# Half of the turned probabilities made by a transposing DMA, exponentials in place over the scores, and weights stored by panel

## The reference

```python
q = (x @ Wq + bq).reshape(1, B * N, H, hd)             # 512 queries, 16 heads of 64
kv = (cond @ Wkv + bkv).reshape(1, -1, 2, H, hd)       # 8192 keys and values
k, v = (kv[:, :, 0], kv[:, :, 1])
q = _fq_sym(q * scale, axis=-1)                        # round to 127 levels per row
k = _fq_sym(k, axis=-1)
v = _fq_sym(v, axis=2)
attn = softmax(einsum('bhqd,bhkd->bhqk', q, k))
attn = _fq_unsigned(attn, axis=-1)                     # round to 255 levels of the row's largest
out = einsum('bhqk,bhkd->bhqd', attn, v)
x1 = out @ Wp + bp
```

## Time and profile before

| What | us |
|---|---|
| Median of three runs | 3053.57 |
| The profiled execution | 3055.36 |
| Its span | 3053.5 |
| Busy: PE, DVE, ACT, POOL | 2747.3, 1967.6, 1139.9, 552.6 |
| Attention, first copy of scores to last output | 1457.32 to 2280.03 |

### The profile page before, as it was taken

How to read it: one execution, slowest core, us unless ns; L and a number is a source line. 1 busy time by engine, 2 the same in 40 slices (tenths; PEclk the granted TensorE clock), 3 DMA queues, 4 the chain that set the end, 5 groups by cost and what they waited for, 6 DMA issues and landing times. The chain is left out here.

```text
span 3053.5 us, 47748 instructions
## 1 busy us (share of the span) xinstructions
PE 2747.3 (90%) x18856; PEld 1408.6 (46%) x18856; DVE 1967.6 (64%) x3074; ACT 1139.9 (37%) x1240; POOL 552.6 (18%) x208
## 2 busy tenths in 40 slices
PE   6999999999999999995788888888867999499998
PEld 3444444444444444443455555555544457244443
DVE  5855555555555555553899999999976344366663
ACT  3111111111111111110699999999983134111100
POOL 0400000000000000000663635353601551001100
PEclk9999999999999999998899999999998986799999
DMA  6122122222122222214323242424213300300000
GB/s 228 62 76 82 57 73 82 82 79 79 65 72 76 82 82 76 73 64 118 104 57 112 57 112 57 112 56 112 57 40 136 111 28 1 59 14 14 8 1 28
DMA packets 241147, 220.14 MB, mean 72 GB/s; under 512 B 137457, under 2 KB 203249, under 8 KB 238193
## 3 DMA queue, kind: packets, MB, share of 16 engines
q1 hardware_dynamic: 241008, 218.06, 22.9%
HBM read 115.28 MB, written 69.21 MB: 60 GB/s over the span
## 5 line engine op out<-in xcount | busy, mean ns | idle before, releaser
L455 PE MATMUL kv_acc<-kv_whi,kv_xthi 128*128 128x512 f16 x2048 | 777.2, 379 | 6.1 <-DVE kv_xtlo L499 6.1
L455 PE MATMUL kv_acc<-kv_wlo,kv_xthi 128*128 128x512 f16 x2048 | 777.2, 379 | 0.0
L455 PE MATMUL kv_acc<-kv_whi,kv_xtlo 128*128 128x512 f16 x2048 | 777.1, 379 | 0.0
L851 DVE TENSOR_SCALAR_CACHE_REDUCE at_sc<-at_score 128x1024 f32<-128x1024 f32 x512 | 608.1, 1217 | 57.7 <-PE at_score L778 57.7
L934 ACT ACTIVATE at_prob<-at_sc,at_bias,at_qs 128x2048 uint16<-128x2048 f32 x256 | 535.2, 2090 | 28.0 <-DVE at_bias L863 26.3
L778 PE MATMUL at_score<-at_kt,at_q 128*128 128x512 f16 x1024 | 317.5, 396 | 141.3 <-DVE at_sc L851 92.2
L486 ACT ACTIVATE kv_parts<-kv_key 128x1024 f16<-128x1024 f32 x64 | 67.7, 1058 | 867.4 <-DVE kv_key L524 867.4
L455 PEld LDWEIGHTS kv_acc<-kv_whi,kv_xthi 128*128 128x128 f16 x2048 | 200.6, 98 | 248.7 <-DVE kv_xtlo L499 6.5
L455 PEld LDWEIGHTS kv_acc<-kv_whi,kv_xtlo 128*128 128x128 f16 x2048 | 200.6, 98 | 242.2 <-issue 1.1
L455 PEld LDWEIGHTS kv_acc<-kv_wlo,kv_xthi 128*128 128x128 f16 x2048 | 200.6, 98 | 242.1 <-issue 1.0
L791 PE MATMUL at_turn<-ident,at_prob 128*128 128x128 f16 x4096 | 279.9, 222 | 31.7 <-DVE at_probt L869 20.8
(11 more groups left out here) (178 smaller groups left out, 3380.9 us busy)
## 6 DMA issues: line engine op xcount, KB each, us to landing
kv_rows<-in_ctx SPq DMA_DIRECT2D x64, 512.0 KB, 6.1
key_rows<-kv_parts SPq DMA_DIRECT2D x64, 512.0 KB, 2.6
values<-kv_val SPq DMA_DIRECT2D x32, 1024.0 KB, 6.3
at_v_raw<-values SPq DMA_DIRECT2D x16, 2048.0 KB, 8.7
wq_stage<-in_wkv SPq DMA_DIRECT2D x4, 2048.0 KB, 8.1
wq_stage<-in_wq SPq DMA_DIRECT2D x2, 2048.0 KB, 13.6
wt_stage<-in_wp SPq DMA_DIRECT2D x2, 2048.0 KB, 10.4
wt_stage<-in_wq SPq DMA_DIRECT2D x2, 2048.0 KB, 8.2
```

The source lines that it names most:

```text
L455: last = nc.tensor.matmul(acc[c][:], a[s][:, k, :], b[:, c, k, :], start=(k == 0 and q == 0), stop=(k == KD - 1 and q == 2))
L851: nc.vector.tensor_scalar(sc[n % 2][:, c * SC:(c + 1) * SC], score[c % 2][:], 1.0, None, ALU.mult, ALU.max, accum_out=part_max[n % 2][:, c ...
```

## The change

1. The four exponentials of 2048 in a slot become two of 4096, and they write in place: the uint16 results lie over the scores that they were made from (`prob` is a view of `sc`). The first half (chunks 0 to 3) lands over chunks 0 and 1, the second over chunks 4 and 5.
2. The first half of the probabilities is no longer turned by PE. A transposing DMA that SP issues (`turn_probabilities`, 128 x 4096 16-bit elements, 1 MB) turns it from SBUF to SBUF, into `probt_dma`, once in each slot. PE sums straight from there (`dma_sums`).
3. The second half is turned by PE as before, four chunks. One is taken out by the DVE and three by ACT, now as plain 16-bit copies; the integers stay in the bit pattern of f16 (so they are 2^-24 of their worth) and the scale of the values is multiplied by 2^24, by one small DVE instruction in `value_scales`.
4. The chunks of scores are made in another order (`ORDER`), and each copy waits for whatever last read the place it writes to: an exponential, PE's turns, or the DMA. All of PE's work that finishes a slot stands one slot later (`finish_slot`), and the output two slots later.
5. The key loads are four transposes of 2048 rows each, placed between the DMAs that turn probabilities. The values are loaded to the room of `x`, which is loaded again at the end of the attention.
6. All weights but those of the feed forward are laid out on the host by panel: each partition gets one run of 16 KB.

The core of the diff:

```diff
-        sp.dma_start(self.stage[n % 2][:], self.sources[n].rearrange("(k p) n -> p k n", p=P))\
+        sp.dma_start(self.stage[n % 2][:], self.sources[n])\
...
+    def keys(self, sp, head, j, quarters):
+        rows, n = self.kt_d.rearrange("u p n -> (u p) n"), NKV // 4
+        for q in quarters:
+            sp.dma_start_transpose(self.kt[j][:, q * n:(q + 1) * n].unsqueeze(1),
+                                   rows[q * n:(q + 1) * n, bass.ds(head * P, P)]).then_inc(self.kt_loaded[j], 16)
...
-    EC = 2048
-    NE = NKV // EC
+    EC = NKV // 2
+    ORDER = (2, 3, 6, 7, 4, 0, 1, 5)
+    BANK = (0, 1, 1, 0)
+    QUARTERS = ((1, 3), (2, 0))
...
-        prob = [chip.sb(ctx, f"at_prob{j}", [P, EC], U16) for j in range(2)]
+        prob = [[sc[j][:].bitcast(U16)[:, at:at + EC] for at in (0, NKV)] for j in range(2)]
+        probt_dma = [chip.sb(ctx, f"at_probt_dma{j}", [P, EC // P, P], F16) for j in range(2)]
...
+            def turn_probabilities(g, n):
+                sp.wait_ge(exp_done, EXP0 + 2 * g + 1)
+                sp.wait_ge(dma_summed, DSUM0 + g + 1 - 2)
+                sp.dma_start_transpose(probt_dma[n % 2][:], prob[n % 2][0].bitcast(F16)).then_inc(dma_turned[n % 2], 16)
...
+            def body(i, first, last):
+                for n in range(SLOTS):
+                    turn_probabilities(i * SLOTS + n, n)
+                    if n % T == T - 1 and not last:
+                        heads.keys(sp, 2 * i + j + 2, j, QUARTERS[0])
+                    if n == 0 and not first:
+                        heads.keys(sp, 2 * i + 1, 1, QUARTERS[1])
+                    if n == T and not last:
+                        heads.keys(sp, 2 * i + 2, 0, QUARTERS[1])
+                    if n == (2 if first else 1):
+                        heads.values(sp, 2 * i + 1)
+                    if n == T + 1 and not last:
+                        heads.values(sp, 2 * i + 2)
...
+            def turns(g, n, k):
+                if k == 0:
+                    pe.wait_ge(exp_done, EXP0 + 2 * g + 2)
+                    pe.wait_ge(out_s, OUT0 + 3 * g)
+                elif k == 2:
+                    pe.wait_ge(out_v, g + 1)
+                elif k == 3:
+                    pe.wait_ge(out_s, OUT0 + 3 * g + 1)
...
+            def dma_sums(i, g, n, half):
+                if half == 0:
+                    pe.wait_ge(dma_turned[n % 2], DMA0 + 16 * (i * (SLOTS // 2) + n // 2 + 1))
...
+            def finish_slot(i, n, c):
+                if c == 0:
+                    turns(g, m, 0)
+                    turns(g, m, 1)
+                elif c == 2:
+                    turns(g, m, 2)
+                elif c == 3:
+                    dma_sums(ii, g, m, 0)
+                elif c == 4:
+                    turns(g, m, 3)
+                elif c == 5:
+                    sums(g, m, 0)
+                    sums(g, m, 1)
+                elif c == 6:
+                    sums(g, m, 2)
+                    sums(g, m, 3)
+                elif c == 7:
+                    dma_sums(ii, g, m, 1)
...
+                if c in (2, 3):
+                    dve.wait_ge(exp_done, EXP0 + 2 * (h - 2) + 1)
+                elif c in (6, 7):
+                    dve.wait_ge(exp_done, EXP0 + 2 * (h - 2) + 2)
+                elif c in (4, 5):
+                    dve.wait_ge(turned, TURNED0 + 4 * (h - 2) + 2 * (c - 4) + 2)
+                else:
+                    dve.wait_ge(dma_turned[n % 2], DMA0 + 16 * (i * (SLOTS // 2) + n // 2))
...
             def body(i, first, last):
                 for n in range(SLOTS):
                     exps(g, n, 0)
                     if not (first and n == 0):
-                        turned_out(g - 1, CH - 1)
-                    for e in range(1, NE):
-                        exps(g, n, e)
-                        turned_out(g, 2 * e - 1)
+                        for k in (0, 2, 3):
+                            turned_out(g - 1, k)
+                    exps(g, n, 1)
...
+            sp.wait_ge(v_quantised, HEADS)
+            sp.dma_start(x[:], x_d).then_inc(chip.rows_loaded, 16)
```

More of the change, by code:

```diff
@@ L44 @@
 NIB_SCALE = 2.0 ** -14
+PROB_UNIT = 2.0 ** 24
 H_SCALE = 2.0 ** -10
@@ L799, in sums @@
                 for b in range(GB):
-                    last = nc.tensor.matmul(outp[n % 2][:, 0:HD], probt[c % 4][:, b, :], v_int[n // T][:, c * GB + b, :],
-                                            start=(c == 0 and b == 0), stop=(c == CH - 1 and b == GB - 1))
+                    last = nc.tensor.matmul(outp[n % 2][:, 0:HD], probt[k][:, b, :], v_int[n // T][:, EC // P + k * GB + b, :],
+                                            start=False, stop=False)
                 last.then_inc(summed, 1)
+            def dma_sums(i, g, n, half):
+                if half == 0:
+                    if n % T == 0:
+                        pe.wait_ge(v_quantised, 2 * i + n // T + 1)
+                    pe.wait_ge(o_taken, TAKEN0 + g + 1 - 2)
+                    pe.wait_ge(dma_turned[n % 2], DMA0 + 16 * (i * (SLOTS // 2) + n // 2 + 1))
+                for b in range(half * 2 * GB, (half + 1) * 2 * GB):
+                    last = nc.tensor.matmul(outp[n % 2][:, 0:HD], probt_dma[n % 2][:, b, :], v_int[n // T][:, b, :],
+                                            start=(b == 0), stop=(b == 4 * GB - 1))
+                if half == 1:
+                    last.then_inc(dma_summed, 1)
@@ L818, in body @@
                                 inputs_ready(i, ahead)
-                            scores(i * SLOTS + ahead, ahead, cc)
-                        if c % 2 == 1:
-                            turns(g, c - 1)
-                            turns(g, c)
-                            if c == 3 and n % T == 0:
-                                pe.wait_ge(v_quantised, 2 * i + n // T + 1)
-                            if c >= 3:
-                                sums(g, n, c - 3)
-                                sums(g, n, c - 2)
-                            elif not (first and n == 0):
-                                sums(g - 1, (n - 1) % SLOTS, CH - 2)
-                                sums(g - 1, (n - 1) % SLOTS, CH - 1)
+                            scores(i * SLOTS + ahead, ahead, pos)
@@ L833, in _ @@
+                        if not (first and n == 0):
+                            finish_slot(i, n, c)
             inputs_ready(0, 0)
@@ L836, in _ @@
             each_pair(pe, body)
-            sums(HEADS * T - 1, SLOTS - 1, CH - 2)
-            sums(HEADS * T - 1, SLOTS - 1, CH - 1)
+            for c in range(CH):
+                finish_slot(PAIRS, 0, c)
         @block.vector
@@ L1389, in halves @@
     def halves(w):
-        return [w[:, h * HALF:(h + 1) * HALF] for h in range(w.shape[1] // HALF)]
+        return [w[h] for h in range(w.shape[0])]
     def cols(n):
```

210 lines of the change are left out of this document (109 added, 101 removed).

## The result

The changed kernel takes **2981.97 us** (median of four, 2981.23 to 2985.34), against 3053.01 (3052.31 to 3053.84) for the kernel before beside it: ratio 0.9766, 95% interval 0.9751 to 0.9781. The prediction was 2953, range 2928 to 2992. Faster is right, the time lies in the range, and it is 29 us off the point. The profiled execution took 2982.49, its span 2980.6.

The account below looks back on a forecast made before the run. DVE bound the old slot at 12.28 us, ACT 3% behind; a ring of waits would set 10.73. Terms -104.2 (first to last bias), +3.3 (tail), +0.2 (extra instruction) made -100.7, giving 2953 us, range 2928 to 2992.

Parts of the forecast that it names:

- The ring: Attention slot: chain of waits through PE, DVE and ACT from one second exponential's end to the next, closing at 10.72 us.
- The exponentials: ACT in each attention slot: two exponentials of 4096 at 3.79 us each, with writing in place taken as 0.
- DVE's floor of 10.48: DVE's own work in an attention slot: copies 9.15, one cast 0.60, small instructions 0.73; the slot's low end, in us.
- ACT's of 10.28: ACT's own work in an attention slot: two exponentials of 3.79 us and three takings out totalling 2.70.
- The threshold of 6.7: SP's DMA queue in the attention: the time of one turn, in us, above which the queue decides the slot.
- The loop edges: Five edges between PE's loop bodies in the attention: the earlier kernel's loss of 18.8 us carried over unchanged.
- The keys' quarters: Key loads at the start: eight issues for two, costing nothing to 2 us; taken as 0.
- The tail: From the last bias to the last output: 18.5 us instead of 15.2, so +3.3.
- The queue that binds: Rival for SP's DMA queue: 7.2 us a turn, 11.25 a slot, +32, total 2985; chance 8%.
- the turning that is slow: Rival: DMA transposes from SBUF at four times the keys' pace, 14.9 us each, slot 18.9, total 3453; chance 9%.
- Waits that miss by a copy: Rival: every wait in PE's order misses by 1.14 us about once a slot; slot 12.3, gain given back; chance 4%.
- The clock: Rival: PE's clock falls to 1.2 GHz in the attention, +3.5 us a slot, 3165 with all slots; chance 4%.

Follow-up runs that it names:

- `exp2048`: The changed kernel with each exponential of 4096 made as two of 2048, still in place, the second waiting for the first: 3046.91 us, ratio 0.9939.
- `best2`: The changed kernel with DVE's taking out earlier, second head's keys later and values sooner, PE's and DVE's attention bodies written out: 2910.93 us, ratio 0.9533.
- `pe_unrolled`: The changed kernel with PE's eight bodies written out, no instruction loop on PE: 2949.09 us, ratio 0.9652.
- `values_early`: The changed kernel with the second head's values asked for after the second turn of probabilities instead of the third: 2978.77 us, ratio 0.9746.
- `key1_later`: The changed kernel with SP asking for the second head's keys at the attention's start instead of the end of the stage before: 2972.1 us, ratio 0.9736.
- `half_turn`: The changed kernel with each DMA turning only the first 2048 of 4096 probabilities, PE summing those blocks twice: 2976.26 us, one execution.
- `turn_and_half`: The changed kernel with a second turning DMA of 2048 probabilities behind each first one, into a buffer nobody reads: 3053.87 us, one execution.

## Why the prediction was right, and where it was off

- *The ring: right.* Its steps are in the timelines within 0.15 us, and three edits moved the slot as it says: -0.33 with the taking out sooner, +0.51 with the second exponential longer, none with half of the DMA. The size was 10.73 and is 10.81 in the written out pairs and 10.88 in the loop (8.4 us). Of this 0.07 is the loop's and goes when PE's is written out; the rest is in the steps of the ring, which come up to 0.15 later than the rows of the kernel before gave.
- *The exponentials: right.* 3.79 predicted, 3.79 measured (3785 to 3801 ns for the 128). Writing in place costs nothing: an exponential of 2048 lasts 2088 ns in place (`exp2048`) and 2090 to another tile (the kernel before). Their size is worth 32 us where PE's clock holds.
- *DVE's floor of 10.48: right.* 10.44 to 10.45 in written out code. ACT's of 10.28 was perhaps too low: in 10.45 it has no gap left (`best2`), with three takings out in 2.87 and not 2.70. But the DVE is as full there, so ACT's floor is 10.45 at most.
- *The DMA: hidden, as predicted*, at 4.92 for a turn where 3.7 was taken. The threshold of 6.7 was not tested closer than between 4.9 (hidden) and 7.4 (slot 12.15).
- *The loop edges: the largest error, 11.7 us.* The step that failed is "PE runs as many loop edges as before: I leave it". PE stands 5.4 us at each, where DVE lost 2.9 and 1.3 before, and behind it the turns that the ring waits for run at half the clock. Before, an edge fell on PE with DVE full and cost 3.9; now it falls into the ring. `pe_unrolled` shows that all of it is PE's loop. PE itself stood 2.9 to 3.4 us at an edge before, and 5.4 to 5.5 now; why its stand is longer is not shown. The 18.8 that was carried over is a little off as well: the distances between the biases give 19.5, and the one edge of the earlier trace rows times five 21.
- *The values of the second head: missed, 4.9 us.* I wrote that the first head's loss goes, which it did, and did not follow the same chain (SP's order, landing, 23 us of POOL) for the second. `values_early` shows the cause.
- *The start: missed, 4.4 us.* "The keys' quarters: nothing to 2 us" was too narrow. SP is held for 26.7 instead of 22.3, and the attention waits for SP's last issue (`key1_later`).
- *The panels: 0 predicted; measured 5.0 less when they came alone,* more than the bound of -2, since they help in two places and I priced one. In the changed kernel the two parts were -2.2 and -2.05.
- *The tail: +3.3 predicted, +5.5 measured.* PE's clock averages 0.67 between the last bias and the last output, where the kernel before had 1.00. The turns that the sum had at full clock run at half: the last 16 take 1.89 us and the last two groups of 8 take 1.03 and 1.04, against 0.62 for 8 in the earlier trace rows.
- *The rivals.* The queue that binds and the turning that is slow both needed more than 4.92 us a turn, and were rightly small. For the latter the Trainium skill's page "VectorE: DVE Perf Modes", section "The three transpose paths", would give 32 x 1309 ns = 41.9 us by an estimate. Here 32 blocks hold SP for 4.92 and have landed after 8.2, so blocks overlap out of SBUF as well. Waits that miss by a copy would have made the slot 12.3, and it was 10.88. The clock was 0.97 and did not bind, but the margin was thinner than 4% says: a slot of 11.39 with the same loop fell into it for two bodies of six.
- *A slip that changed nothing.* The distance from the first bias to the last holds 63 slots and not 62; the sum for the new kernel does not use that count (61 x 10.73 and 20.2 for the other two, which lasted 20.5).
- *The range: part luck.* Its upper side was 30 us for costs of writing in place and for waits that miss, and neither came. The time went up by the edges, which the range had only at full or half their price, by the second head's values and by the start, for which it had nothing. That their sum stayed inside is not a merit of the bounds.

The short form: the mechanism was right. The span came out 27.8 us above the sum (72.9 less and not 100.7): 8.4 are the size of the slot, 11.7 the edges, 4.9 the values, 4.5 the start, 2.2 the tail, and the panels gave some 4 back.

## What to carry to other kernels

When an engine's full row is emptied by a change, follow the ring of waits that is left, in order, with the times of one slot. If no engine is full afterwards, a swap of two instructions of the engine that both ends wait for may be worth more than a faster instruction (here 20 us for one moved line). Price each loop edge anew whenever the ring passes through the engine that has it: an edge is a standstill and then a slower clock, and writing out one engine's loop took all of it away in the changed kernel (33 us). In the kernel before the same edit took 19 us from the attention, and the whole gained 5. A term that was seen once, for the first head, has to be followed for every head that meets the same queue.

## What the hardware showed that was not expected

- PE's low clock can come back in every slot. The same slot lasted 11.39 at a granted clock of 1.00 or 13.68 at 0.75, for seven slots on end, and each kind began and ended at an edge of PE's loop (`exp2048`).
- A turning DMA's hold on SP is not in proportion to its size: 1.87 us for 2048 columns (`half_turn`) and 4.92 for 4096 (medians of 64 each; the shortest are 1.32 and 4.70). It grows with the load of the queue: 5.36 for 4096 in `turn_and_half`.
- The profile's busy share of the DMA engines is no measure of room: at 0.95 every turn was hidden, and it can pass 1 (1.12, where they were not).
- Apart from its edges, the loop on PE costs 0.07 to 0.08 us a slot and that on DVE 0.10, on slots of 10.5 to 10.9. What in the loop costs it (waits and addresses that are computed in registers, perhaps) is not shown.
